# Another order of the steps on all engines of a two-layer gated block, with two waits moved

## The chip, the cores and the metric

The kernel runs on one core of a Trainium2 chip. The metric is the device time of one execution in microseconds. The kernel before takes 654.42 us (median of 3 runs, 654.09 to 656.05).

## The reference

The input is x of 16 sequences with 128 tokens and 256 channels, and a context of 16 x 128 x 64. Two layers follow each other; in each, an attention over the context and a feed-forward network are added to x behind a gate tanh(g), both after a layer norm without weights.

```python
x = x + tanh(g_xattn[0]) * (softmax(q k^T / 4) v @ Wc.T + bc)     # 16 heads of 16, 4 groups of keys
x = x + tanh(g_ffn[0]) * (sparsify_2to4(silu(n @ w_gate) * (n @ w_up)) @ w_down)    # 1024 wide
x = x + tanh(g_xattn[1]) * (softmax(q k^T / sqrt(8)) v)           # 32 heads of 8, 8 groups
x = x + tanh(g_ffn[1]) * (sum over 8 experts of cw * expert(n) + shared expert(n))  # 176 wide
```

q is the normalised x itself, k and v are the context. sparsify_2to4 keeps the two largest of each four. cw holds, for the two experts with the largest biased score, sqrt(softplus(n @ gate_w.T)), and 0 for the rest.

## The kernel before, in words

**Units.** The work is cut into 32 units, one sequence in one layer each. The order of units is a list: four of layer 0, then one of layer 1 and one of layer 0 in turn, then the last four of layer 1. A *pair* is one unit of either layer. What follows calls the unit that comes first "unit 0"; units 0 to 3 are the first four sequences in layer 0.

**Steps.** Each unit's program on an engine is written as four generators (attention_1, attention_2, ffn_1, ffn_2), which yield between steps. `merge` (in front of the engines' programs) gives each step the time 20000·n + t, with n the unit's number in the list and t from the table `TIMES`, sorts all steps of an engine by it, and emits them in that order. The engines run their instructions in this order and wait on semaphores for each other, so `TIMES` sets nothing but the order on each engine. SP's order is not in the table; it is written out at the end of SP's program.

```python
                    steps += [(SLOT * n + t, n, h, run) for t in TIMES[name][h, L]]
            steps += [(TIMES[name][part.__name__][0], -1, 0, part()) for part in once]
            for *_, run in sorted(steps, key=lambda s: s[:3]):
                next(run, None)
```

**TensorE (PE).** In attention_1 it transposes q (L750) and makes the scores for the row maxima (L789); in attention_2 it makes the transposed scores (L818, L819 in layer 0, L821 in layer 1), the weighted sums (L832, 8 or 16 matmuls), turns the result, and in layer 0 projects it (`product`, L742 to L745). In ffn_1 it turns the normalised rows into UP[0], waits for their rounded part and the rest (f_at_hi from ACT L673, f_at_lo from VectorE L1182) in a step of its own (L883 and L884), and makes the gate and up products, in layer 1 those of the shared expert and the router first (L907 to L911). In ffn_2 it turns the hidden rows (hT0, hT1, ..), makes the other experts' products and the down products. Products are in rounded float32, with a rounded part ("hi") and the rest ("lo") of the operands, so that each is two or three matmuls.

**ACT and VectorE (DVE).** ACT copies from PSUM with rounding, takes exponentials (L658) and silu, and for the router Abs and Relu (L689, L690), Exp (L693) and Ln (L696); `prepare`, `round_keys`, `round_up` (L606) and `round_down` (L614) round the weights once. Between Exp, Ln and Silu stands a table load. ao_hi (L666) is the rounded part of the attention's result. VectorE takes maxima (L1092), norms, the low parts, the hidden products; `split_keys` (L1037), `split_up` (L1044) and `split_down` (L1053) make the low parts of the weights once.

**POOL.** It computes reciprocal roots, the low part of q (L471, q_lo), x + b (L480), copies of the values (L485, L493), small router steps, the drop of the sparse values (L515), sets constants (`late_constants`, L436 to L449), and issues two loads on its own DMA queue: `load_w13` (L561, all experts' first weights, 3168 KB) and `load_w2` (L567, L569).

**Keys.** The keys k are rounded and split once. For units 0 and 1 SP copies them straight into place (`first_k0`, L299 and L301). For all others SP first writes them to a scratch in DRAM (`stage_keys`: kd0a twice, L338, kd0b, L340, kd1, L343, with the 1 MB load of w_down, L341, in between) and reads each unit's part from there (`load_k0`, L306 and L308). SP does unit 0's next loads, then stage_keys, then unit 1's next loads and unit 2's keys; before stage_keys it waits until unit 0's value copy on POOL is done (v0_done), because the next load overwrites its source.

Of the kernel before, what the change touches and what calls it, by code (L numbers as in the profile page):

```python
# [31 lines left out]
def flamingo_block(nc, x, ctx_kv, ctx_t, g_x, g_f, wc_t, bc, w_up, w_down, gate_w_t, gate_b, w13, w2, out):  # L32
# [22 lines left out]
    with ctx:  # L55
# [130 lines left out]
        def wait_part(eng, name, n, k):  # L186
# [3 lines left out]
        SLOT = 20000  # L190
        TIMES = {
            "Pool": {
                (0, 0): [-12726, -11933, -8176, 2795, 4595],
                (0, 1): [-14992, -14516, -10388, -1699],
                (1, 0): [19249],
                (1, 1): [20461],
                (2, 0): [36844, 36845, 48715, 48716, 53506],
                (2, 1): [36843, 36844, 39683, 39684, 39685, 40505, 41937, 41938, 41939],
                (3, 0): [57067, 57628, 58227],
                (3, 1): [58491],  # L200
                "one_hot_1": [-11725],
                "late_constants": [24996],
                "load_w13": [61],
                "load_w2": [80360],
            },
            "Act": {
                (0, 0): [521, 2075, 5158],
                (0, 1): [867, 868, 4047, 4048],
                (1, 0): [17463, 19059, 21601, 22294, 25145, 27473, 34511, 36218],
                (1, 1): [18686, 18758, 22595, 23037, 27030, 29353, 30610, 31365, 31366, 31430, 34845, 35181],  # L210
                (2, 0): [48564, 54697, 56775, 59277, 61858],
                (2, 1): [49748, 54795, 55454, 56580, 58664, 59330],
                (3, 0): [60865, 74180, 75237],
                (3, 1): [59488, 61027, 74290, 75390, 75654, 75655, 78503],
                "prepare": [2709],
                "round_keys": [5972],
                "round_up": [38364],
                "round_down": [56819],
            },
# [9 lines left out]
            },  # L229
            "DVE": {  # L230
# [8 lines left out]
                "prepare": [-3234],  # L239
                "split_keys": [17241],  # L240
                "split_up": [41480],
                "split_down": [60289],
            },
        }

# [490 lines left out]
        def _(pe):  # L736
# [127 lines left out]
            def ffn_1(i, L):  # L864
# [15 lines left out]
                wait(pe, "f_norm", n)  # L880
                turn(UP[0], lambda k: f_xn[:, P * k:P * (k + 1)], KT).then_inc(S["f_xt_ps"], 1)
                yield
                wait(pe, "f_at_hi", n)  # L883
                wait(pe, "f_at_lo", n)  # L884
                if L == 0:
                    for c in range(2):
                        yield
                        for b_, off, name in ((0, 0, "f_g"), (1, I0, "f_u")):
                            if b_:
                                yield  # L890
                            if c:
                                wait(pe, "f_h0" if b_ else "f_sg0", n)
                            for k in range(KT):
                                if k:
                                    yield
                                w = slice(off + CH * c, off + CH * (c + 1))
                                last = product(UP[b_][:, :], at_hi[b][:, k, :], at_lo[b][:, k, :],
                                               up_hi[:, k, w], up_lo[:, k, w], k == 0, k == KT - 1)
                            last.then_inc(S[f"{name}{c}"], 1)
                else:  # L900

                    yield
                    c0 = 2 * E * EI
                    for k in range(KT):
                        if k:
# [399 lines left out]
```

## Time and profile before

| | |
|---|---|
| median of 3 runs | 654.42 us |
| profiled execution | 653.18 us |
| its span, first to last instruction | 651.4 us |
| mean granted clock of PE | 0.982 |
| PE busy | 582.7 us, 89% of the span |
| DVE, ACT, POOL busy | 471.9, 436.8, 238.8 us |
| DMA | 21.44 MB, mean 33 GB/s |

The profile is of one execution. A busy time is the sum of an engine's instructions; a wait is an engine's idle time with what ended it. Matmuls overlap in the pipeline, so the spacing of their starts tells more than their durations. The granted clock is a share of 2.4 GHz, and 0.50 is the level of 1.2 GHz. Queue q1 is SP's, q10 is ACT's, q0 is POOL's; all of them run on the core's 16 DMA engines.

### The profile page before, as it was taken

What the parts mean: (1) busy time and instruction counts of PE and PEld (TensorE: products, weight loads), DVE (VectorE), ACT (ScalarE), POOL (GpSimd) and SP (SyncE); (2) the same over time, 40 slices, a digit from 0 to 9 for tenths busy, and PEclk for the clock granted to TensorE, in tenths of its full rate; (3) what the DMA queues carried; (4) which work ended last, traced back from release to release, by engine and by line L of the source; (5) the groups of instructions that cost most, each with busy time, mean ns of one, the idle gap of its engine ahead of it and who ended that gap; (6) DMA issues with size and microseconds to landing.
All of it is one profiled execution on the core that took longest, in us unless ns stands there. A gap on an engine that the chain in (4) does not pass through costs nothing.

```text
span 651.4 us, 10817 instructions
## 1 busy us (share of the span) xinstructions
PE 582.7 (89%) x3552; PEld 450.7 (69%) x3552; DVE 471.9 (72%) x1152; ACT 436.8 (67%) x812; POOL 238.8 (37%) x498
## 2 busy tenths in 40 slices
PE   0654788999999999999999999999999999999886
PEld 0332576777878777777878787777778786767675
DVE  4361878686969788796969697887969696966444
ACT  3251655677786877677777868776777778678952
POOL 5340444261534334251515343351515152341120
PEclk9975999899999999999999999999999999999999
DMA  8752007000000000000000000000000000000000
GB/s 258 217 183 75 4 17 109 18 9 18 14 21 10 22 15 18 10 18 17 17 19 15 20 9 22 14 15 12 18 9 11 8 11 10 12 7 2 10 8 17
DMA packets 24694, 21.44 MB, mean 33 GB/s; under 512 B 9872, under 2 KB 23680, under 8 KB 23744
## 3 DMA queue, kind: packets, MB, share of 16 engines
q1 hardware_dynamic: 21984, 13.04, 7.8%
q0 software_dynamic: 1888, 4.87, 2.5%
q10 hardware_dynamic: 768, 2.85, 1.5%
q8 instruction: 29, 0.48, 0.3%
q14 instruction: 25, 0.20, 0.1%
HBM read 12.61 MB, written 5.24 MB: 27 GB/s over the span
## 4 chain that ended last, share of the span: by engine, by line
PE 66%; ACT 13%; POOL 7%; DVE 6%; issue 5%; DMA 2%; SPq 1%; DVEq 0%; POOLq 0%; ACTq 0%
PE bank L742 12%; PE bank L750 12%; PE bank L745 12%; PE bank L789 8%; PE bank L832 7%; PE bank L744 5%; PE bank L821 4%; ACT L658 3%; POOL rt L547 3%; ACT L696 2%; ACT pt L658 2%; PE bank L818 2%; PE bank L819 2%; DMA k0a<-down_hi 2%; PE bank L911 1%
## 5 line engine op out<-in xcount | busy, mean ns | idle before, releaser
L658 ACT ACTIVATE pt<-bank 128x512 f32<-128x512 f32 x192 | 109.4, 603 | 10.1 <-PE bank L821 5.5
L1092 DVE TENSOR_REDUCE mx<-bank 128x4 f32<-128x512 f32 x128 | 86.1, 684 | 8.3 <-PE bank L789 7.4
L707 ACT ACTIVATE ht_hi<-bank 128x512 fp32r<-128x512 f32 (+1 forms) x96 | 50.4, 543 | 61.4 <-PE bank L750 60.8
L742 PE MATMUL bank<-w_r,at_hi 128*128 128x352 f32 x256 | 88.4, 346 | 3.4 <-DVE work L1200 0.9
L456 POOL TENSOR_SCALAR a_ve<-a_mv 128x1 f32<-128x1 f32 x32 | 9.1, 284 | 214.2 <-DVE a_mv L1062 213.3
L745 PE MATMUL bank<-w_r,at_lo 128*128 128x352 f32 x256 | 82.2, 323 | 0.0
L1137 DVE SCALAR_TENSOR_TENSOR work<-bank,cw,work 128x176 f32<-128x176 f32 x128 | 45.3, 395 | 42.5 <-ACT work L724 28.4
L1092 DVE TENSOR_REDUCE q0b<-bank 128x4 f32<-128x512 f32 x64 | 42.6, 688 | 42.3 <-PE bank L789 42.0
L1231 DVE TENSOR_TENSOR ht_lo<-bank,ht_hi 128x512 fp32r<-128x512 f32 (+1 forms) x96 | 58.0, 618 | 18.4 <-ACT ht_hi L707 18.4
L821 PE MATMUL bank<-qt,k 128*128 128x512 f32 x128 | 54.1, 443 | 7.4 <-DMA qt<-mt 3.3
L742 PEld LDWEIGHTS bank<-w_r,at_hi 128*128 128x128 f32 x256 | 48.4, 189 | 15.3 <-DVE work L1200 5.8
L742 PE MATMUL bank<-up_hi,at_hi 128*128 128x512 f32 x128 | 55.5, 434 | 0.0
L750 PE MATMUL bank<-ident,work 128*128 128x128 f32 x336 | 50.5, 275 | 4.5 <-DVE work L1137 2.5
L789 PE MATMUL bank<-k,qt 128*128 128x512 f32 x128 | 49.7, 426 | 2.2 <-ACT qt L642 1.7
L744 PE MATMUL bank<-up_lo,at_hi 128*128 128x512 f32 x128 | 50.9, 397 | 0.0
L745 PE MATMUL bank<-up_hi,at_lo 128*128 128x512 f32 x128 | 50.7, 396 | 0.0
L742 PE MATMUL bank<-w_r,ht_hi 128*128 128x256 f32 x208 | 50.2, 281 | 0.0
L745 PE MATMUL bank<-w_r,ht_lo 128*128 128x256 f32 x208 | 49.9, 279 | 0.0
L745 PEld LDWEIGHTS bank<-w_r,at_lo 128*128 128x128 f32 x256 | 48.2, 188 | 1.9
L750 PEld LDWEIGHTS bank<-ident,work 128*128 128x128 f32 x336 | 40.2, 141 | 13.4 <-DVE work L1137 3.7
L832 PE MATMUL bank<-pt,v 128*32 128x512 f32 x384 | 48.8, 611 | 0.0
L515 POOL TENSOR_TENSOR work<-work,keep 128x512 f32<-128x512 f32 x32 | 37.3, 1165 | 25.0 <-DVE keep L1168 25.0
(163 smaller groups left out, 1540.7 us busy)
## 6 DMA issues: line engine op xcount, KB each, us to landing
w_r<-in_w POOLq DMA_DIRECT2D x1, 3168.0 KB, 13.8
x<-in_x SPq DMA_DIRECT2D x16, 128.0 KB, 2.2
work<-in_w_up ACTq DMA_DIRECT2D x2, 1024.0 KB, 9.3
k<-kd SPq DMA_DIRECT2D x128, 12.0 KB
out<-y SPq DMA_DIRECT2D x16, 128.0 KB, 1.7
w_r<-in_w POOLq DMA_DIRECT2D x1, 1536.0 KB, 7.1
kd0a<-down_hi SPq DMA_DIRECT2D x2, 512.0 KB
pt<-in_w_down SPq DMA_DIRECT2D x1, 1024.0 KB, 19.3
```

Source lines behind the costliest of these rows:

```text
L658: act.activation(pt[:, g, :], PV[g % 2][:, :], ACT.Exp, scale=float(HD[L]) ** -0.5)\
L707: act.activation(ht_hi[:, 4 * t:4 * t + cols // P, :], DOWN[b][:, 0:cols].rearrange("p (k t) -> p k t", t=P), ACT.Copy)\
L742: pe.matmul(o, a_hi, w_hi, start=first, stop=False, skip_group_check=free)
L744: pe.matmul(o, a_hi, w_lo, start=False, stop=False, skip_group_check=free)
L745: return pe.matmul(o, a_lo, w_hi, start=False, stop=last, skip_group_check=free)
L750: last = pe.transpose(o[:, P * k:P * (k + 1)], src(k), ident[:, :])
L789: pe.matmul(QK[(1 + m) % 2][:, :], qt[b][:, t, P * j:P * (j + 1)], k_[:, 4 * t:4 * t + 4, :].rearrange("p g t -> p (g t)"), start=True, st ...
L821: last = pe.matmul(o, k1[c][:, g, :], qt[b][:, g // 4, :], start=True, stop=True)
L832: last = pe.matmul(PV[0][BLK * g:BLK * (g + 1), :], vv[:, 4 * t + g, :], pt[:, 4 * t + g, :], start=t == 0, stop=t == tiles - 1, skip_grou ...
L1092: dve.tensor_reduce(o, QK[(1 + m) % 2][:, :].rearrange("p (g t) -> p g t", t=T), AX.X, ALU.max, negate=True).then_inc(S["a_r"], step)
L1137: last = dve.scalar_tensor_tensor(out=hid[b][:, EI * e:EI * (e + 1)], in0=o[:, EI * k:EI * (k + 1)], scalar=cw[b][:, e:e + 1], in1=sg[b][: ...
L1231: dve.tensor_tensor(ht_lo[:, r, :], DOWN[b][:, 0:cols].rearrange("p (k t) -> p k t", t=P), ht_hi[:, r, :].bitcast(F32), ALU.subtract).then ...
```

## The change

The table `TIMES` gets other numbers, so that the order changes on PE, ACT, DVE and POOL. The two waits of PE for the split rows move from a step of their own to the step of the first product that reads them. No operation is added or removed. The part of the table that the text speaks of, and the moved waits:

```diff
         TIMES = {
             "Pool": {
-                (0, 0): [-12726, -11933, -8176, 2795, 4595],
-                (0, 1): [-14992, -14516, -10388, -1699],
+                (0, 0): [-15000, -14999, -10496, -1576, -1575],
+                (0, 1): [-12565, -12564, -9814, -5533],
...
-                "one_hot_1": [-11725],
-                "late_constants": [24996],
-                "load_w13": [61],
-                "load_w2": [80360],
+                "one_hot_1": [-14199],
+                "late_constants": [-7829],
+                "load_w13": [16839],
+                "load_w2": [22346],
...
             "Act": {
...
-                (1, 0): [17463, 19059, 21601, 22294, 25145, 27473, 34511, 36218],
+                (1, 0): [11579, 16631, 18206, 20385, 21777, 22019, 24894, 29235],
...
-                (2, 1): [49748, 54795, 55454, 56580, 58664, 59330],
+                (2, 1): [42225, 47367, 51807, 53210, 55296, 56805],
...
-                "prepare": [2709],
-                "round_keys": [5972],
-                "round_up": [38364],
-                "round_down": [56819],
+                "prepare": [1023],
+                "round_keys": [7257],
+                "round_up": [12373],
+                "round_down": [45546],
...
             "PE": {
-                (0, 0): [-559, 1533, 1773, 3821, 8011],
+                (0, 0): [-3011, 3429, 4743, 6848, 8003],
...
-                (1, 0): [12633, 16179, 17889, 19242, 20545, 22954, 25084, 28315, 30810, 30811],
+                (1, 0): [13189, 13757, 15851, 17195, 20380, 22309, 26401, 27950, 30027, 30300],
...
-                (2, 0): [40913, 43206, 43207, 44676, 46174, 50799, 51022, 52507, 52737, 53443],
-                (2, 1): [41823, 44672, 44836, 44837, 52109, 52264, 56478, 56479],
-                (3, 0): [62720, 62721, 67431, 67482, 69795, 69922, 70871],
+                (2, 0): [41161, 44330, 45550, 47182, 49606, 49786, 51148, 52503, 53285, 53383],
+                (2, 1): [41709, 44728, 45305, 47205, 51933, 52514, 55943, 55944],
+                (3, 0): [57444, 60603, 67366, 67649, 68973, 70573, 70574],
...
             "DVE": {
...
-                "prepare": [-3234],
-                "split_keys": [17241],
-                "split_up": [41480],
-                "split_down": [60289],
+                "prepare": [-2515],
+                "split_keys": [13618],
+                "split_up": [22778],
+                "split_down": [58931],
...
                 turn(UP[0], lambda k: f_xn[:, P * k:P * (k + 1)], KT).then_inc(S["f_xt_ps"], 1)
                 yield
-                wait(pe, "f_at_hi", n)
-                wait(pe, "f_at_lo", n)
                 if L == 0:
                     for c in range(2):
                         yield
+                        if c == 0:
+                            wait(pe, "f_at_hi", n)
+                            wait(pe, "f_at_lo", n)
...
                 else:
 
                     yield
+                    wait(pe, "f_at_hi", n)
+                    wait(pe, "f_at_lo", n)
```

Read as an order, with the steps at the start in which the two kernels differ most:

- POOL before: unit 0's root and q_lo, load_w13, unit 0's x + b and values, unit 1's root, q_lo, x + b and values, late_constants, unit 2. After: unit 0's root and q_lo, late_constants, unit 0's x + b and values, unit 1's root and q_lo, load_w13, unit 1's x + b and values, load_w2, unit 2. Before, load_w2 stands where the fifth unit begins.
- ACT before: round_up stands behind unit 0's ao_hi, round_down in unit 0's ffn_1, behind unit 1's ao_hi. After: round_up stands ahead of unit 0's attention_2, round_down between unit 1's attention result and its ao_hi.
- DVE before: split_keys behind unit 1's normalisation, split_up ahead of unit 0's second normalisation. After: split_keys ahead of unit 1's normalisation, split_up behind it and ahead of unit 1's maxima.
- PE before: unit 2's first two score products stand ahead of unit 1's weighted sums. After: behind them.
- In a pair later on, PE before: layer 0's last transposed scores, then the new layer 1 unit's first two score products, its turned rows and the old unit's first turned hidden half. After: that half directly behind the transposed scores. ACT before: Abs and Relu of the router, the second half's rounding, the router's Exp, ao_hi, Ln. After: the second half's rounding, Abs and Relu, ao_hi, Exp, Ln.

## Rows read from the trace of the kernel before

**Rows 1.** Busy time by stage; then PE's granted clock, DMA share, GB/s
```profile
42.50:58.00 15.50, 3.36 (x10) 1.74 (x10) 4.74 (x6) 2.77 (x6) 4.89 (x5) 0.61 0.41 135
80.00:540.00 460.00, 447.54 (x2802) 353.46 (x2801) 363.57 (x898) 331.37 (x623) 183.06 (x375) 1.00 0.08 18
540.00:651.40 111.40, 96.82 (x605) 74.88 (x604) 68.36 (x185) 74.34 (x140) 26.80 (x62) 1.00 0.03 9
```

**Rows 2.** The chain of waits, 0 to 80 us: start us, us, what
```profile
9.17 11.04 DMA k0a<-down_hi
...
47.94 10.12 issue
```

**Rows 3.** Timeline of SP's queue: start us, us of issuing, operation
```profile
18.30 0.59 SPq L301 DMA_DIRECT2D k0b<-down_lo  x1
...
24.70 1.26 SPq L338 DMA_DIRECT2D kd0a<-down_hi  x2
...
47.70 1.20 SPq L306 DMA_DIRECT2D k0a<-kd0a  x1
```

**Rows 4.** DMA queues, 14 to 22 us: packets, MB, share of 16 engines
```profile
q0 software_dynamic: 244, 3.09, 95.3%
q1 hardware_dynamic: 244, 0.15, 24.3%
q10 hardware_dynamic: 141, 0.04, 9.4%
```

**Rows 5.** DMA queues, 22 to 24 us
```profile
q1 hardware_dynamic: 638, 0.16, 37.2%
```

**Rows 6.** DMA queues, 26 to 28 us
```profile
q1 hardware_dynamic: 14, 0.11, 26.7%
```

**Rows 7.** DMA issues: what, KB each, us from issue to landing
```profile
w_r<-in_w POOLq DMA_DIRECT2D x1, 3168.0 KB, 13.8
...
w_r<-in_w POOLq DMA_DIRECT2D x1, 1536.0 KB, 7.1
```

**Rows 8.** Timelines of DVE and ACT: weights split and rounded; start us, us
```profile
40.81 4.99 DVE L1044 TENSOR_TENSOR up_lo<-work,up_hi 128x2048 fp32r<-128x2048 f32 x2
...
67.53 1.90 ACT L614 ACTIVATE down_hi<-pt 128x2048 fp32r<-128x2048 f32 x1
```

**Rows 9.** Timeline of PE behind the second gate; idle time before in brackets
```profile
59.19 1.94 PE L832 MATMUL bank<-pt,v 128*32 128x512 f32 x8
...
73.17 0.50 PE L818 MATMUL bank<-qt,k0a 128*128 128x512 f32 x1 [1.57 <-ACT pt L658]
...
77.52 0.41 PE L750 MATMUL bank<-ident,f_xn 128*128 128x128 f32 x2 [2.31 <-DVE f_xn L1066]
```

**Rows 10.** Timeline of PE, one pair of units
```profile
313.91 0.40 PE L818 MATMUL bank<-qt,k0a 128*128 128x512 f32 x1
314.14 0.40 PE L819 MATMUL bank<-qt,k0b 128*128 128x512 f32 x1
314.58 0.70 PE L789 MATMUL bank<-k,qt 128*128 128x512 f32 x2
...
350.42 0.70 PE L789 MATMUL bank<-k,qt 128*128 128x512 f32 x2
```

**Rows 11.** Waits of PE's weight loads, 160 to 520 us: us, times, longest
```profile
PEld bank L821 <- DMA qt<-mt: 5.3, 10, 0.5
...
PEld bank L742 <- DVE work L1200: 3.9, 10, 0.4
PEld bank L821 <- ACT pt L658: 3.4, 10, 0.4
```

**Rows 12.** Timeline of ACT, the router of one unit
```profile
320.23 0.20 ACT L693 ACTIVATE rt<-rt 128x8 f32<-128x8 f32 x1
320.89 0.38 ACT L666 ACTIVATE ao_hi<-bank 128x256 fp32r<-128x256 f32 x1 [0.46 <-PE bank L750]
321.30 1.28 ACT L696 ACT_TABLE_LOAD   x1
```

More of the change, by code:

```diff
@@ L192, in flamingo_block @@
             "Pool": {
-                (0, 0): [-12726, -11933, -8176, 2795, 4595],
-                (0, 1): [-14992, -14516, -10388, -1699],
[L195 to L200, printed above, removed]
-                "one_hot_1": [-11725],
-                "late_constants": [24996],
@@ L203, in flamingo_block @@
-                "load_w13": [61],
-                "load_w2": [80360],
+                (0, 0): [-15000, -14999, -10496, -1576, -1575],
+                (0, 1): [-12565, -12564, -9814, -5533],
+                (1, 0): [18632],
+                (1, 1): [11838],
+                (2, 0): [31094, 31095, 47595, 49321, 50573],
+                (2, 1): [30923, 30924, 37097, 37098, 37289, 37438, 37589, 41658, 43145],
+                (3, 0): [55922, 56685, 56686],
+                (3, 1): [50053],
+                "one_hot_1": [-14199],
@@ L205, in flamingo_block @@
+                "late_constants": [-7829],
+                "load_w13": [16839],
+                "load_w2": [22346],
             },
             "Act": {
-                (0, 0): [521, 2075, 5158],
-                (0, 1): [867, 868, 4047, 4048],
-                (1, 0): [17463, 19059, 21601, 22294, 25145, 27473, 34511, 36218],
-                (1, 1): [18686, 18758, 22595, 23037, 27030, 29353, 30610, 31365, 31366, 31430, 34845, 35181],
-                (2, 0): [48564, 54697, 56775, 59277, 61858],
@@ L212, in flamingo_block @@
-                (2, 1): [49748, 54795, 55454, 56580, 58664, 59330],
-                (3, 0): [60865, 74180, 75237],
-                (3, 1): [59488, 61027, 74290, 75390, 75654, 75655, 78503],
-                "prepare": [2709],
-                "round_keys": [5972],
-                "round_up": [38364],
-                "round_down": [56819],
+                (0, 0): [-2525, -2524, 2141],
+                (0, 1): [-2580, -1918, 1054, 1178],
+                (1, 0): [11579, 16631, 18206, 20385, 21777, 22019, 24894, 29235],
@@ new lines, in flamingo_block @@
+                (1, 1): [11053, 16063, 19285, 22101, 22212, 22832, 24053, 24054, 25522, 25758, 27915, 28572],
+                (2, 0): [42310, 50008, 53019, 56531, 58415],
+                (2, 1): [42225, 47367, 51807, 53210, 55296, 56805],
+                (3, 0): [59841, 63075, 66082],
+                (3, 1): [57130, 58962, 65811, 68905, 71876, 72168, 73704],
+                "prepare": [1023],
+                "round_keys": [7257],
+                "round_up": [12373],
+                "round_down": [45546],
```

22 rows, old and new, of the table TIMES are left out of this document.

## The prediction, made before the changed kernel ran

> **What bounds the kernel now.** I read the busy times by stage first, then the chain of waits of the start and the DMA queues there, and last one period of the steady stage.
>
> TensorE is the engine with the least idle time, and that idle time is what can be won. The stages tell where it lies [rows 1]: from 80 to 540 us it lacks 460 − 447.5 = 12.5 us, at the end 14.6 us, and in the 15.5 us before 58 us it works for 3.4 us only. The chain of the start names two gates [rows 2]: 11.04 us until the first unit's keys land (TensorE resumes at about 20.3 us), and 10.12 us in which TensorE waits, until 58.06 us, for the keys of the third unit, the first that come back from the scratch in DRAM.
>
> The second gate is a queue. SP issues the last piece of unit 1's keys at 18.30 us, but the first copy of all keys to the scratch only at 24.70 us and the third unit's keys at 47.70 us [rows 3]; they stand behind the copies and the 1 MB of the down projection. What such a queue does beside another one shows in the stage from 14 to 22 us, when the big expert load (w13, 3168 KB) runs on POOL's queue: 244 packets of it moved, and 244 packets of SP's queue [rows 4]. The DMA engines take turns, one packet each, whatever their size. A w13 packet held an engine for 0.953·8·16/244 = 0.50 us; as soon as w13 had landed, SP's queue moved 638 packets in 2 us [rows 5].
>
> The copy to the scratch does not use all engines: from 26 to 28 us, when it runs alone, 14 packets took 26.7% of 16 engines, that is 4.3 engines at 0.61 us a packet [rows 6]. So a mean DMA share of 0.41 before the gate [rows 1] may be a few engines that are never free.
>
> **The change, part by part.** It reorders the steps; no operation is added or taken away, the matmuls and table loads stay as many.
>
> *First gate.* On POOL, w13 moves from before unit 0's sum x+b to behind unit 1's q_lo, so that by the walk it is issued at about 24 us instead of ahead of the first gate. The up weights are through by 14 us (ACT's queue moved only 0.04 MB after that [rows 4]). Some 200 packets of the first keys, a part of the 244 and 141 of SP's and ACT's queues, were then left, and with nothing big to take turns with they need under 1 us [rows 5]: the gate opens at about 15.4 us, −4.9 us. SP gains the same: unit 0's value copy no longer waits for a late load, and SP goes on at 18.9 us, where its own issuing ends. The key copies start at 19.8 instead of 24.70 us: −4.9 us. Three more steps go ahead here and are counted at nothing: the late constants on POOL, because unit 0's value copy must only be done by 18.9 us; rounding the up weights on ACT, because its next step waits for unit 0's last maximum, near 19 us; the split of the keys ahead of unit 1's normalisation, because TensorE has the third unit's keys to wait for in the end. If that wait went, they would cost some 5 us of unit 1's start.
>
> *w13 beside the key copies.* This is what the move pays. w13 now runs from about 29 us, in the middle of the copies. It has 3168 KB in 256 rows of 12.4 KB, a packet each, 16 an engine. On an engine that the copies keep busy, each takes its 0.50 us out of turn: +8.0 us. Ends: 0, if the copies' engines have gaps enough, and 8.0. I take 8.0: packet for packet is what [rows 4] show.
>
> *w2 beside them.* The second expert load moves from far behind, where the fifth unit begins, to close behind w13. It is 1536 KB in 1 KB packets and took 7.1 us from issue to landing [rows 7], on all engines. Behind w13 in its queue it meets the rest of the copies, the down weights and the keys, packet for packet: between 0 and 7.1 us, and I take 4.0, since on the busy engines most of what it meets is left by then.
>
> The gate before the third unit's keys thus goes from 58.06 to 58.06 − 4.9 + 8.0 + 4.0 = 65.2 us: **+7.1 us**. SP's queue is behind in any case; TensorE, with less to wait for earlier, stands there from about 43 us.
>
> The Trainium skill ("DMA: Bandwidth & Descriptors", section on queues, rings and completion order) says that each engine goes round its queues by packets, which agrees with the equal counts. In its section on why a semaphore rises by 16 it says that a DMA from SP uses as many engines, up to 16, as divide the outer dimension on both sides: four for the copy with four groups outside, and the 4.3 engines agree. Its fit of 2.0 us plus bytes over 436 GB/s would give, as an estimate, 10.9 us of transfer for both loads spread over all engines, and with that in place of the 12.0 us the kernel would come to 656.4 us.
>
> *Behind the gate.* The weighted sums of unit 1 now stand before the gate, in the wait. They took 1.94 us [rows 9] right behind a stretch with a mean granted clock of 0.61 [rows 1]; I count half of it, for at the gate other products run at that clock in their place. Rounding the down weights, 1.90 us on ACT [rows 8], moves into the wait too; it held up the exponentials for which TensorE waited 1.57 us. The next wait, 2.31 us for unit 1's normalised rows [rows 9], hangs on VectorE's chain with the split of the down weights in it, which stays where it was; so the two don't add. What is late next is this chain, and it starts about 1.4 us sooner: −1.4 us, between 0 and −3.5. Splitting the up weights, 4.99 us on VectorE [rows 8], goes ahead of the gate; its cover is the wait for the keys, and without that cover it would cost those 5 us at unit 1's maxima.
>
> *Steady stage.* A pair of units takes 350.42 − 314.58 = 35.84 us [rows 10]; 80 to 540 us is 12.8 pairs. Small waits stand in each: for the maxima's row by DMA 0.5, VectorE's product 0.4, the exponentials 0.3 [rows 11], and 0.2 us ahead of a unit's first scores (314.58 − 314.14 = 0.44, where such products follow each other by 0.23 [rows 10]); 1.4 us a pair. Walking through the new order with these durations: the turn of the old unit's hidden half now stands before the new unit's first scores and fills one (−0.2); unit 1's q moves ahead of two products and a tie of VectorE ahead of the normalisation, which fills some of the third (−0.2). Against it, the router's exponential moves behind ao_hi on ACT: it ran at 320.23, and the table load at 321.30 followed ao_hi directly [rows 12]; now its 0.20 us come in between, on the chain that ends in the first and second wait (+0.15). The two waits of TensorE, for the split rows, now stand at the first product that reads them. Left at their own step they would hold the two score products that the new order puts in between, and with them the maxima on VectorE; by themselves they give nothing, for in the old order next to nothing stood there. Sum −0.2 a pair, **−2.6 us** in all; at best the whole 1.4 us a pair, −18 us; at worst one more 0.5 us wait a pair, +6.4 us.
>
> *End.* The last units keep their order but for neighbours: 0, ±1.5 us.
>
> **Sum:** +7.1 − 1.4 − 2.6 = +3.1 us. The profiled execution's span of 651.4 becomes 654.5 us, with the 1.8 us around it 656.3; the median of the three runs stands 1.2 us over that execution (654.42 to 653.18), so 657.5 us.
>
> **The rivals.**
> (a) *The loads fit into free engine time, faster.* The mean DMA share of 0.41 before the gate speaks for it, the 4.3 engines against it. Then 8.0 and 4.0 vanish, the gate is at 53.2 us, and the time is 654.42 − 4.9 − 1.4 − 2.6 = 645.5 us. It decides if less than 6.9 of the 12 us are in the way: below that the kernel is faster by over 0.3%. Chance 0.15 for all of it, 0.08 for about half (651.5).
> (b) *The new order takes out half of the steady waits*, −9.5 instead of −2.6: 650.6 us. For it: TensorE's producers have room (ACT works for 331 and VectorE for 364 of 460 us [rows 1]). Against: their waits hang on chains, not on load. 0.12.
> (c) *ACT's chain gets late*: the exponential behind ao_hi, and the wait at the product that needs sgs grows by 0.5 us a pair: +6.4 instead of −2.6, 666.5 us. 0.13.
> (d) *The order changes nothing that binds* in the steady stage; the start alone gives 660.1 us. That belongs to my forecast's spread.
>
> **How the numbers follow.** The forecast with its spread (654 to 661) has 0.52. A measurement tells apart about 0.3%, 2.0 us. Of the forecast 0.35 are slower, 0.16 the same, 0.01 faster; (c) is slower; (a) is faster, its half mostly the same or faster; (b) is faster or the same. Faster 0.28, same 0.24, slower 0.48. The range of 8 in 10 leaves out (a) in full and the far end of (c): 648 to 664 us.
>
> **What would show it.** Right: TensorE's first scores near 15.4 us; w13 issued near 24 us; TensorE idle from about 43 to 65 us, with the third unit's keys landing last; in the stage of that wait POOL's and SP's queues with equal packet counts; 2 us or more less idle behind the gate; a pair of 35.4 to 35.9 us. Wrong: a gate before 58 us (then the copies' engines had room), or a pair shorter than 35.2 or longer than 36.2 us.

## The result, and the profile after the change

The changed kernel takes 658.04 us (median of 6 runs, 657.44 to 658.61) where the kernel before takes 655.77 us (6 runs, 654.09 to 656.84): a ratio of 1.0039, 95% interval 1.0022 to 1.0055. It is 2.3 us slower; 3.1 us had been forecast.

The traced executions are further apart, since that of before (653.18 us) is shorter than any of its six runs: spans of 651.4 and 656.3 us. Where the 4.9 us between them arise can be read off three products that both traces have: the third unit's first scores, and the weighted sums of the sixth and of the 28th unit, 11 pairs apart.

| from | to | before | after | difference |
|---|---|---|---|---|
| start | third unit's first scores | 58.06 us | 66.89 us | +8.8 us |
| these | sixth unit's weighted sums | 78.62 us | 76.09 us | -2.5 us |
| these | 28th unit's weighted sums | 394.40 us | 392.18 us | -2.2 us |
| these | end of the span | 120.3 us | 121.1 us | +0.8 us |

The timelines that the table is made from. TensorE before (L832 is the weighted sum, and the third unit's scores stand in the chain of [rows 2]):

```profile
136.68 1.06 PE L832 MATMUL bank<-pt,v 128*32 128x512 f32 x8
...
531.08 1.07 PE L832 MATMUL bank<-pt,v 128*32 128x512 f32 x8
```

After:

```profile
16.59 1.19 PE L789 MATMUL bank<-k0a,qt 128*128 128x512 f32 x2 [5.06 <-DMA k0a<-down_hi]
...
66.89 1.19 PE L789 MATMUL bank<-k0a,qt 128*128 128x512 f32 x2 [21.36 <-issue]
...
142.98 1.06 PE L832 MATMUL bank<-pt,v 128*32 128x512 f32 x8
...
535.16 1.06 PE L832 MATMUL bank<-pt,v 128*32 128x512 f32 x8
```

The reader sees the first gate open at 16.59 instead of 20.30 us, and the second at 66.89 instead of 58.06 us: TensorE now stands there for 21.36 us (10.12 before, [rows 2]). "Issue" is what the profile calls a wait for which it finds no releaser; the last of the third unit's keys lands at 66.80 us, 0.09 us earlier. The timeline of SP's queue after the change, to be held against [rows 3]:

```profile
20.00 1.26 SPq L338 DMA_DIRECT2D kd0a<-down_hi  x2
...
25.99 19.53 SPq L343 DMA_DIRECT2D kd<-down_hi  x2
...
52.08 2.03 SPq L306 DMA_DIRECT2D k0a<-kd0a  x1
```

And POOL's timeline, with the issues of w13 and of the larger part of w2:

```profile
26.95 0.98 POOL L561 DMA_DIRECT2D w_r<-in_w  x1
...
29.88 1.06 POOL L567 DMA_DIRECT2D w_r<-in_w  x1
```

SP starts the copies of the keys 4.7 us earlier, but the first read of the third unit's keys is issued 4.4 us later. In between SP takes 19.53 us to issue two of the copies to kd1 (11.74 us before); the profile does not say why, and that its queue took no more is a reading. The stages, against [rows 1] (PE's granted clock is the third number from the right):

```profile
42.50:58.00 15.50, 2.62 (x13) 0.96 (x11) 0.42 (x1) 2.56 (x5) 0.00 (x0) 0.61 0.63 176
58.00:66.00 8.00, 0.00 (x0) 0.00 (x0) 0.00 (x0) 1.82 (x1) 0.00 (x0) 0.50 0.35 94
...
80.00:540.00 460.00, 446.66 (x2794) 352.10 (x2793) 363.36 (x901) 330.85 (x625) 183.96 (x373) 0.99 0.05 15
540.00:656.30 116.30, 103.07 (x637) 80.88 (x635) 73.18 (x192) 78.41 (x147) 30.05 (x68) 0.99 0.03 9
```

From 58 to 66 us every engine stands but ACT, which rounds the down weights (L614) from 64.18 us on, while the DMA engines are busy for 0.35 of the time only. That a few of them have most of the work fits the 4.3 engines of [rows 6], but it is argued: the profile does not say on which engine a packet ran. The DMA queues after the change from 32 to 36 us, in the middle of w13 (packets, MB, share of 16 engines):

```profile
q0 software_dynamic: 103, 1.31, 81.6%
q1 hardware_dynamic: 34, 0.23, 21.5%
```

The counts are not equal as in [rows 4]: at least 69 of w13's packets took no turns with SP's. Nor are they equal in TensorE's wait itself: from 45.5 to 66.9 us POOL's queue moved 452 packets, most of them of w2, and SP's 2075.

A pair of units on TensorE's timeline, against [rows 10]:

```profile
319.73 0.40 PE L819 MATMUL bank<-qt,k0b 128*128 128x512 f32 x1
319.96 0.60 PE L750 MATMUL bank<-ident,work 128*128 128x128 f32 x4
320.32 0.71 PE L789 MATMUL bank<-k,qt 128*128 128x512 f32 x2
...
355.96 0.71 PE L789 MATMUL bank<-k,qt 128*128 128x512 f32 x2
```

ACT's timeline in the router, against [rows 12]:

```profile
326.19 0.38 ACT L666 ACTIVATE ao_hi<-bank 128x256 fp32r<-128x256 f32 x1 [0.43 <-PE bank L750]
326.47 0.20 ACT L693 ACTIVATE rt<-rt 128x8 f32<-128x8 f32 x1
326.69 1.28 ACT L696 ACT_TABLE_LOAD   x1
```

The turn of the old unit's hidden half starts 0.23 us after the last transposed scores, as one such product after the other, and the new unit's scores follow it 0.36 us later: the slack in the 0.44 us of [rows 10] is filled. On ACT the Exp (L693) now stands between ao_hi and the table load. A pair takes 355.96 - 320.32 = 35.64 us instead of 35.84.

### The profile page after: what moved, and what is told of

The parts are those of the page before. It is cut to its first block, busy times and chain, and to the rows that moved or that the text cites. A ratio compares the mean times of both kernels' runs of the same rounds, so it can differ in the third digit from the quotient of the medians.

```text
span 656.3 us, 10816 instructions
## 1 busy us (share of the span) xinstructions
PE 583.3 (89%) x3552; PEld 454.9 (69%) x3552; DVE 471.3 (72%) x1152; ACT 436.1 (66%) x812; POOL 240.6 (37%) x498
## 4 chain that ended last, share of the span: by engine, by line
PE 64%; DVE 11%; POOL 9%; ACT 8%; issue 6%; DMA 1%; SPq 1%; DVEq 0%; POOLq 0%; ACTq 0%
PE bank L750 12%; PE bank L742 12%; PE bank L745 11%; PE bank L832 7%; PE bank L789 7%; PE bank L744 5%; PE bank L821 3%; POOL rt L547 3%; ACT L696 2%; PE bank L818 2%; PE bank L819 2%; DVE work L1140 2%; DVE f_xn L1069 2%; POOL a_rs L459 1%; PE bank L914 1%
## 5 line engine op out<-in xcount | busy, mean ns | idle before, releaser
L456 POOL TENSOR_SCALAR a_ve<-a_mv 128x1 f32<-128x1 f32 x32 | 10.6, 332 | 232.3 <-DVE a_mv L1065 231.3
L742 PE MATMUL bank<-w_r,at_hi 128*128 128x352 f32 x256 | 90.3, 354 | 4.6 <-DVE work L1203 1.0
L1095 DVE TENSOR_REDUCE mx<-bank 128x4 f32<-128x512 f32 x128 | 83.8, 677 | 9.6 <-PE bank L789 9.5
L745 PE MATMUL bank<-w_r,at_lo 128*128 128x352 f32 x256 | 82.1, 322 | 0.0
L1140 DVE SCALAR_TENSOR_TENSOR work<-bank,cw,work 128x176 f32<-128x176 f32 x128 | 45.3, 396 | 40.5 <-ACT work L724 27.0
L821 PE MATMUL bank<-qt,k 128*128 128x512 f32 x128 | 56.7, 446 | 4.9 <-DMA qt<-mt 3.1
L750 PE MATMUL bank<-ident,work 128*128 128x128 f32 x336 | 53.0, 277 | 4.9 <-DVE work L1140 3.0
L789 PE MATMUL bank<-k,qt 128*128 128x512 f32 x128 | 51.1, 440 | 1.0 <-ACT qt L642 0.6
L832 PE MATMUL bank<-pt,v 128*32 128x512 f32 x384 | 48.7, 609 | 1.8 <-ACT pt L658 1.6
L789 PE MATMUL bank<-k0a,qt 128*128 128x512 f32 x64 | 25.8, 448 | 27.0 <-issue 21.4
```

The source lines that it names most:

```text
L742: pe.matmul(o, a_hi, w_hi, start=first, stop=False, skip_group_check=free)
L745: return pe.matmul(o, a_lo, w_hi, start=False, stop=last, skip_group_check=free)
L750: last = pe.transpose(o[:, P * k:P * (k + 1)], src(k), ident[:, :])
L789: pe.matmul(QK[(1 + m) % 2][:, :], qt[b][:, t, P * j:P * (j + 1)], k_[:, 4 * t:4 * t + 4, :].rearrange("p g t -> p (g t)"), start=True, st ...
L821: last = pe.matmul(o, k1[c][:, g, :], qt[b][:, g // 4, :], start=True, stop=True)
L832: last = pe.matmul(PV[0][BLK * g:BLK * (g + 1), :], vv[:, 4 * t + g, :], pt[:, 4 * t + g, :], start=t == 0, stop=t == tiles - 1, skip_grou ...
```

## The experiments

The theory was the prediction's: the two expert loads beside the copies of the keys make the second gate late, the new order of the other engines gains a little, and the balance is the difference of the two. The rivals were that the loads fit into free engine time, that the order makes the gate late, and that single steps are worth other amounts than the sum had. They ran in three groups, each on one chip. The kernel before, run beside them, spread from 648.2 to 658.9 us there (medians 653.43, 653.02 and 652.96 us; beside the result its six runs lay within 2.8 us), so times tell apart a few us only; for fractions of a us the traces are read: the gate is the start of the third unit's first scores, and a pair is 1/11 of the time between the weighted sums of the sixth and the 28th unit.

| kernel | us | ratio to before (95%) | gate, us | pair, us |
|---|---|---|---|---|
| old_order_new_loads | 661.19 | 1.0111 (1.0057 to 1.0165) | 64.25 | 35.84 |
| new_order_old_loads | 647.16 | 0.9895 (0.9844 to 0.9947) | 56.75 | 35.64 |
| new_order_w2_back | 650.94 | 0.9969 (0.9941 to 0.9997) | 61.25 | 35.64 |
| new_order_w13_late | 644.71 | 0.9865 (0.9816 to 0.9915) | 53.47 | 35.63 |
| late_waits_own_step | 651.03 | 0.9954 (0.9921 to 0.9986) | 54.94 | 36.07 |
| late_hT0_back | 649.21 | 0.9942 (0.9903 to 0.9981) | 54.65 | 35.81 |
| late_exp_ahead | 652.45 | 0.9975 (0.9939 to 1.0012) | 54.49 | 35.54 |
| late_keys_split | 634.17 | 0.9724 (0.9675 to 0.9773) | 45.32 | 35.63 |
| changed_keys_split | 642.92 | 0.9855 (0.9798 to 0.9912) | 52.31 | 35.64 |
| old_keys_split | 642.11 | 0.9843 (0.9783 to 0.9903) | 48.45 | 35.85 |
| old_w13_behind_xb | 650.66 | 0.9966 (0.9923 to 1.0009) | 53.16 | 35.86 |
| split_exp_ahead | 632.03 | 0.9681 (0.9614 to 0.9748) | 45.69 | 35.54 |

### Loads and order apart

The old order with the loads at their new steps:

```diff
-                "late_constants": [24996],
-                "load_w13": [61],
-                "load_w2": [80360],
+                "late_constants": [60],
+                "load_w13": [12000],
+                "load_w2": [24996],
```

> The order of the kernel before; only the three POOL steps (late constants, w13, w2) stand where the change puts them. Theory (the two expert loads beside the key copies make the second gate, whatever the order): first scores near 16.6 us, third unit's keys land near 66.9 us as after the change (58.06 before), a pair stays at 35.85 us, time 655.8 + 8.8 = 664.6 us (663 to 667). Rival (the new order of the other engines makes the late gate, the loads fit in free engine time): gate at 53 us, 650 us.

The new order with both loads at their old steps:

```diff
-                "load_w13": [16839],
-                "load_w2": [22346],
+                "load_w13": [-9000],
+                "load_w2": [80360],
```

> The changed kernel with both expert loads back at their old places (w13 behind unit 0's q_lo, w2 where the fifth unit begins). Theory: first scores near 20.3 us, third unit's keys at 58.1 us, behind that the order's own gain of 1.4 us and 0.2 us a pair: 655.8 - 4.0 = 651.8 us (649 to 653). Rival (the new order gains nothing, the trace of after just stood high or low): 655.8 us.

The new order with w2 alone put back:

```diff
-                "load_w2": [22346],
+                "load_w2": [80360],
```

> The changed kernel with w2 alone back where the fifth unit begins; w13 stays behind unit 1's q_lo. Theory of the prediction's sum (w13 costs 8.0 us and w2 4.0): third unit's keys at 66.9 - 4.0 = 62.9 us, 654.0 us. Rival A (w2 is nothing, it uses idle engines): 658 us. Rival B (w2's small packets cost its full 7.1 us): 651 us.

And the new order with w2 back and w13 behind unit 3's value copy:

```diff
-                "load_w13": [16839],
-                "load_w2": [22346],
+                "load_w13": [58426],
+                "load_w2": [80360],
```

> The changed kernel with w13 issued behind unit 3's value copy (about 89 us, its first product stands at 144 us) and w2 at its old place. Theory: first scores near 16 us, key copies alone from 20 us as they ran from 24.7 us before, so the third unit's keys at 58.1 - 4.7 = 53.4 us and the time 658.0 - 13.5 = 644.5 us (643 to 648). Rival (the copies are late by themselves, or w13 beside the loads of later units holds those up): 650 us or more.

The third unit's first scores on TensorE's timeline (its wait in brackets), in old_order_new_loads:

```profile
64.25 1.19 PE L789 MATMUL bank<-k0a,qt 128*128 128x512 f32 x2 [19.89 <-issue]
```

In new_order_old_loads:

```profile
56.75 1.19 PE L789 MATMUL bank<-k0a,qt 128*128 128x512 f32 x2 [11.57 <-issue]
```

In new_order_w2_back:

```profile
61.25 1.19 PE L789 MATMUL bank<-k0a,qt 128*128 128x512 f32 x2 [15.25 <-issue]
```

In new_order_w13_late:

```profile
53.47 1.19 PE L789 MATMUL bank<-k0a,qt 128*128 128x512 f32 x2 [5.28 <-issue]
```

The gate goes with the loads, under either order. In the new order, taking w2 away from the copies moves it from 66.89 to 61.25 us: w2 costs 5.6 us. Taking w13 away too moves it to 53.47: w13 costs 7.8 us. What is left is the copies themselves: 33.5 us from their first issue (19.99 us) to the gate, as in the kernel before (24.70 to 58.06, 33.4 us). In times the loads cost 661.19 - 653.43 = 7.8 us in the old order, and the order gains 653.43 - 647.16 = 6.3 us with the old loads; the interval has the 4.0 us expected in it. Of the 6.3 us, 1.3 are the gate, at 56.75 instead of 58.06 us: the key copies start at 21.82 us there. That rival (a) is wrong is shown by this. With both loads out of the way the changed kernel is faster than the one before by 1.35%.

Two runs did not come out as expected. The gate and the time of old_order_new_loads are lower than the 66.9 us and 663 to 667 us: with the loads at the same steps and the key copies from 20.0 us on, the gate is at 64.25 us in the old order and at 66.89 in the new one. So the new order does make the gate later, by 2.6 us. POOL comes to w13 at 25.14 us in the old order and at 26.95 in the new one; that this is the reason was not tested. Against old_w13_behind_xb (below), whose copies start at 20.05 us, the two loads cost the old order 64.25 - 53.16 = 11.1 us at the gate, not 13.4. And the 650.94 us of new_order_w2_back are rival B's 651 us rather than the 654.0 us of the theory; its gate, with 5.6 us, lies between the two, and the kernel before ran 2.3 us shorter on that chip than beside the result.

### The order's parts in a pair

Three kernels undo one step each, on the base of new_order_w13_late. TensorE's waits in a step of their own again (in either layer):

```diff
                 yield
+                wait(pe, "f_at_hi", n)
+                wait(pe, "f_at_lo", n)
                 if L == 0:
                     for c in range(2):
                         yield
-                        if c == 0:
-                            wait(pe, "f_at_hi", n)
-                            wait(pe, "f_at_lo", n)
...
                     yield
-                    wait(pe, "f_at_hi", n)
-                    wait(pe, "f_at_lo", n)
```

> Base is the changed kernel with both loads late (pair 35.63 us, 8.7 us under the kernel before). Here TensorE's two waits for the split rows stand again in a step of their own. Theory of the prediction (left there they hold the score products that the new order puts in between, and the maxima behind them): a pair of 35.7 to 36.0 us, 1 to 5 us slower than the base. Rival (split rows are ready by then, moving the waits is worth nothing): a pair of 35.63 us, same time as the base.

The turned hidden half behind the new unit's first scores (TensorE, layer 0):

```diff
-                (3, 0): [57444, 60603, 67366, 67649, 68973, 70573, 70574],
+                (3, 0): [57444, 61710, 67366, 67649, 68973, 70573, 70574],
```

> Same base; one step of TensorE goes back: the old unit's first turned hidden half stands behind the new unit's first two scores and turned rows, as before the change. Theory (that turn fills the 0.2 us ahead of a unit's first scores): a pair of 35.83 us, as the kernel before, 2.6 us slower than the base. Rival (the 0.2 us a pair come from other places of the order): a pair of 35.63 us.

The router's Abs, Relu and Exp ahead (ACT, layer 1):

```diff
-                (2, 1): [42225, 47367, 51807, 53210, 55296, 56805],
+                (2, 1): [42225, 46000, 48000, 53210, 55296, 56805],
```

> Same base; on ACT the router's Abs, Relu and Exp stand again ahead of ao_hi (Abs and Relu ahead of the second half's rounding too), as before the change. Theory of the prediction (Exp behind ao_hi costs 0.15 us a pair on the chain to the maxima's row and the shared silu): a pair of 35.48 us, 1.9 us faster than the base. Rival (Exp there lies on no chain that binds): a pair of 35.63 us, same time.

The weighted sums on TensorE's timeline that bound the 11 pairs, in the base, new_order_w13_late:

```profile
127.33 1.06 PE L832 MATMUL bank<-pt,v 128*32 128x512 f32 x8
...
519.23 1.07 PE L832 MATMUL bank<-pt,v 128*32 128x512 f32 x8
```

In late_waits_own_step:

```profile
132.01 1.06 PE L832 MATMUL bank<-pt,v 128*32 128x512 f32 x8
...
528.82 1.06 PE L832 MATMUL bank<-pt,v 128*32 128x512 f32 x8
```

In late_hT0_back:

```profile
133.66 1.06 PE L832 MATMUL bank<-pt,v 128*32 128x512 f32 x8
...
527.62 1.06 PE L832 MATMUL bank<-pt,v 128*32 128x512 f32 x8
```

In late_exp_ahead:

```profile
130.92 1.06 PE L832 MATMUL bank<-pt,v 128*32 128x512 f32 x8
...
521.82 1.07 PE L832 MATMUL bank<-pt,v 128*32 128x512 f32 x8
```

Against the base's 391.90 / 11 = 35.63 us, the hidden half back costs 0.19 us a pair, where the whole change gains 0.20. As the later Exp costs 0.09 us (below), other steps must give about 0.1 us a pair; the prediction's other gain, unit 1's q and the tie of VectorE (0.2 us), was not tested. The waits in their own step cost 0.44 us a pair (36.07 us, just over the 35.7 to 36.0 expected), more than the new order gains; the view of the weight loads' waits of late_waits_own_step, from 160 to 520 us (us, times, longest), names the place, the score products, two in each pair. The base has no such row; the kernel before has it with 13.0 us, so it gives the place and not the amount:

```profile
PEld bank L789 <- issue: 8.2, 20, 0.5
```

So in the new order the moved waits are what makes the rest pay; moved alone, in the old order, they were not run. The Exp ahead gains 0.09 us a pair (0.15 had been expected), yet the kernel got slower, not faster, and its trace says where: 81.0 us from the weighted sums of the 28th to those of the last unit instead of 78.0, and 48.2 instead of 41.7 us of span behind these. ACT's timeline of late_exp_ahead in the last units:

```profile
605.44 1.28 ACT L693 ACT_TABLE_LOAD   x1
...
606.96 1.28 ACT L724 ACT_TABLE_LOAD   x1
...
612.14 1.28 ACT L696 ACT_TABLE_LOAD   x1
```

And TensorE's waits there from 540 us on (us, times, longest):

```profile
PE bank L750 <- DVE work L1140: 9.2, 4, 3.1
```

In the last units, where no unit of layer 0 runs beside, the step Exp had moved ahead of a silu of the unit before it: Exp, silu, Ln, each with a table load, 17 loads ahead of that silu instead of 14. One number serves all units of a layer, and what helps in a pair hurts at the end. TensorE's wait in that row is 3.0 us in the base.

### What the copies of the keys cost by themselves

```diff
                 for a in range(2):
-                    sp.dma_start(kd0a[:, a], kh.bitcast(F32)).then_inc(S["scratch_k0"], 16)
+                    for g in range(G0):
+                        sp.dma_start(kd0a[g, a], kh[HD0 * g:HD0 * (g + 1), :].bitcast(F32))\
+                            .then_inc(S["scratch_k0"], 16)
...
-                sp.wait_ge(S["scratch_k0"], 16 * 3)
+                sp.wait_ge(S["scratch_k0"], 16 * (2 * G0 + 1))
```

The same edit was put on three kernels: on new_order_w13_late,

> Same base; each of the two copies of the keys to kd0a is issued as four DMAs, one for each group of keys, instead of one with the four groups outside. Theory (the copy of four groups keeps about four DMA engines busy, and these are the gate; a copy of one group's 16 rows spreads over all): third unit's keys land at 41 to 47 us instead of 53.4, TensorE, which has work until 44.5 us, hardly waits, 7 to 9 us faster than the base. Rival (the memory or the queue bounds the copies, not the number of engines): gate stays at 52 to 54 us.

on the changed kernel as it is,

> The changed kernel as it is (w13 issued at about 27 us, w2 at 30), with each copy of the keys to kd0a issued as four DMAs. With both loads late the same split put the landing of the third unit's keys at 43.6 us and the time 2.8% under the kernel before. Theory (on a DMA engine that has key packets waiting the loads' packets go in turn, w13's 16 of 0.50 us among them): the loads still cost most of their 13.4 us, keys land at 52 to 57 us, 643 to 648 us on a chip where the kernel before takes 653. Rival (the loads cost only because about four engines were overfull; on even engines they fit in between): keys land at 44 to 47 us, 634 to 638 us.

and on the kernel before:

> The kernel before, only with each copy of the keys to kd0a issued as four DMAs. Theory: the second gate was these copies' four engines; from the first copy's issue at 24.7 us the third unit's keys need 23.6 us as in the split kernel with late loads (20.0 to 43.6), so they land at 48 us and TensorE, which comes there at 47.9 us, does not wait: 9 to 10 us faster than the kernel before. Rival (w13 until 23 us has already delayed everything else that TensorE waits for there): 3 us faster or less.

The timeline of SP's queue in late_keys_split:

```profile
20.01 4.46 SPq L339 DMA_DIRECT2D kd0a<-down_hi  x8
...
32.70 1.51 SPq L306 DMA_DIRECT2D k0a<-kd0a  x1
```

Its DMA queues from 24 to 26 us:

```profile
q1 hardware_dynamic: 82, 0.34, 74.5%
```

The third unit's first scores on its TensorE:

```profile
45.32 0.73 PE L791 MATMUL bank<-k0a,qt 128*128 128x512 f32 x2
```

The same in changed_keys_split:

```profile
52.31 1.19 PE L791 MATMUL bank<-k0a,qt 128*128 128x512 f32 x2 [6.94 <-issue]
```

And in old_keys_split:

```profile
48.45 1.19 PE L791 MATMUL bank<-k0a,qt 128*128 128x512 f32 x2 [0.24 <-issue]
```

Issued by groups, the copies to kd0a land between 20.0 and 27.3 us; as two DMAs they took from 20.0 to 40.5 us in the base. They moved 0.11 MB in 2 us with 26.7% of the engines' time [rows 6], and now 0.34 MB with 74.5%. SP issues on 10.5 us earlier, TensorE's wait is gone, and the kernel is 2.8% faster than before, where the base is 1.35% faster. The rule of the Trainium skill that the prediction cites ("DMA: Bandwidth & Descriptors", section on why a DMA increments its semaphore by 16) is borne out: 16 rows outside use more engines than four groups. The loads, put beside the split copies again, cost 52.31 - 45.32 = 7.0 us at the gate, and more of the keys themselves: the third unit's land at 52.22 instead of 43.57 us, 8.7 us later, part of it hidden by TensorE's work until 45.3 us. So they are not free here either, though they cost about two thirds of their 13.4 us. The copies to kd1, with eight groups outside, were split in no run; an even load of all engines was not tested. In the kernel before, the split alone takes away 9.6 us of the gate, and TensorE hardly waits there any more (0.24 us).

### The first gate

```diff
-                "load_w13": [61],
+                "load_w13": [2796],
```

> The kernel before, only with w13 one step later on POOL, behind unit 0's x+b: its issue goes from 9.58 to about 11 us, its first packet from 13.9 to about 15.5. Theory (the first gate is a race of w13's first packets with the first keys, which cannot flow before the up weights are through at about 14.6 us; w13 needs no large move): first scores at 16.4 us instead of 20.3, key copies issued at 22 to 23 us, third unit's keys at 56 to 57 us, 1 to 2 us faster. Rival (w13 holds the keys up wherever it is issued in this stretch): first scores at 20 us or later, no faster.

First scores and gate of this kernel on TensorE:

```profile
16.56 1.19 PE L789 MATMUL bank<-k0a,qt 128*128 128x512 f32 x2 [5.02 <-DMA k0a<-down_hi]
...
53.16 1.19 PE L789 MATMUL bank<-k0a,qt 128*128 128x512 f32 x2 [9.18 <-issue]
```

The first gate opens at 16.56 us, as expected; the key copies start at 20.05 us already (22 to 23 expected), and the second gate is earlier than expected (56 to 57). The median is 2.3 us lower, but the interval reaches over 1, so in time this is inconclusive. Two other runs show that the gate of 20.30 us is not even a property of the kernel before. old_keys_split has the same instructions as before up to 24 us, w13 at its old step among them. Its POOL issues w13 here:

```profile
10.25 0.98 POOL L563 DMA_DIRECT2D w_r<-in_w  x1
```

And its TensorE has the first scores here:

```profile
17.05 1.19 PE L791 MATMUL bank<-k0a,qt 128*128 128x512 f32 x2 [5.51 <-DMA k0a<-down_hi]
```

ACT issued its DMAs 0.6 us slower in that execution, so q_lo and with it w13 came at 10.25 instead of 9.58 us and its first packet at 14.60 instead of 13.94 us, when the keys had already been let through. new_order_old_loads, with w13 at 10.24 us, has its first scores at 16.35 us. So of the three traces with w13 at its old step only one has the late first gate, and whether it was the one step on POOL that opened it in old_w13_behind_xb stays open. How often the kernel before falls on either side was not measured; it would be one reason for its spread.

### Both gains together

The split copies, both loads late, and Exp ahead of ao_hi but so close that no silu of the last units comes between Exp and Ln:

```diff
-                (2, 1): [42225, 47367, 51807, 53210, 55296, 56805],
+                (2, 1): [42225, 46000, 49000, 53210, 55296, 56805],
```

> The changed kernel with both loads late and the copies to kd0a split (634.2 us), and on ACT the router's Abs, Relu and Exp ahead of ao_hi, but Exp close ahead of it, so that in the last four units no silu stands between Exp and Ln (the run with Exp further ahead had 17 instead of 14 table loads ahead of the shared silu, all three in the last units). Theory (Exp ahead of ao_hi is worth 0.09 us a pair; those three table loads and the waits behind them were what that run lost at its end): pair 35.54 us, 14 such table loads, 633 us. Rival (the early Exp itself delays the last units): pair 35.54 us and 636 us or more.

The weighted sums on its TensorE that bound the 11 pairs:

```profile
119.67 1.06 PE L834 MATMUL bank<-pt,v 128*32 128x512 f32 x8
...
510.59 1.06 PE L834 MATMUL bank<-pt,v 128*32 128x512 f32 x8
```

A pair of 35.54 us and 14 such table loads, 632.03 us: 3.2% under the kernel before, and the fastest of all. The Exp itself does not delay the last units: from the weighted sums of the 28th to those of the last it takes 78.0 us, and 42.9 us behind these (78.0 and 43.1 in late_keys_split). Beside late_keys_split (634.17 us, 2 runs) the 2.1 us are near the 1.0 us that 11 pairs make, but within the scatter.

## Why the prediction was right

**First gate, -4.9 us.** Right for SP (24.70 to 20.00, -4.7), short for TensorE (20.30 to 16.59, -3.7, where 15.4 us was forecast), and wrong in its cause for TensorE. The step that failed is "the gate opens at about 15.4 us" because w13 is gone: with w13 back at its old step it opens at 16.35 us. By the traces the 20.30 us of before was a race lost by some 0.6 us, which is argued. For the sum this did not matter, since the second gate hangs on SP.

**w13, +8.0 us.** Measured 7.8, in the new order; w13 was issued at 26.95 us (24 expected). The packet count was right, and so was its condition, an engine that the copies keep busy. The sign named for it was wrong: elsewhere w13 ran alone (103 against 34 packets), so the equal counts were not there. That its packets waited in turn on the copies' engines is argued, from 7.8 against 16 x 0.50 us.

**w2, +4.0 us.** Mis-sized: 5.6 us, inside the bounds of 0 and 7.1. With w13 that makes 13.4 us for both in the new order and 11.1 us in the old one, where the sum had 12.0. The prediction's estimate by the fit of the Trainium skill ("DMA: Bandwidth & Descriptors", section on the anatomy of one DMA), 10.9 us (11.05 by the KB of [rows 7]), is further off in the new order and nearer in the old one; it is for loads spread over all engines, and the copies that they meet are not spread.

**The gate** was to come at 65.2 us and came at 66.89, and TensorE stood from 45.5 us on (43 expected).

**Behind the gate, -1.4 us.** Measured -2.5, inside 0 to -3.5, but not the same with every place of the loads. With the old loads it is 78.62 to 76.25 us (new_order_old_loads), -2.4. With the new loads it is 82.05 (old_order_new_loads, 64.25 to 146.30 us) to 76.09 us: -6.0, beyond the range. The sum counted the order at nothing at the gate, where it costs 2.6 us, and at too little behind it, where it had not priced the granted clock either (below). These misses run against each other, so that +2.3 us came out beside +3.1 is in part luck.

**Steady stage, -0.2 us a pair.** Measured 0.20, and the parts that were tested were nearly right: 0.19 for the hidden half (0.2), 0.09 lost by the Exp (0.15). The third part, 0.2 us by unit 1's q and the tie, was not tested; the sum leaves it about 0.1. That the waits at the first product save the score products of the new order was right, with 0.44 us a pair as its size; that they give nothing by themselves is not shown.

**End, 0 +- 1.5 us.** +0.8.

Of the rivals, (a) is excluded by the load experiments, (b) and (c) by the pair of 35.64 us, (d) by its 0.20 us. Half of 1.4 us in 12.8 pairs is 9.0 us and not the 9.5 of (b); this changes nothing.

## What to carry to other kernels

Before a big load is moved "out of the way", look at what its queue will meet at the new place: beside copies that keep a few DMA engines full, w13 cost 7.8 us, nearly its 16 x 0.50 us of packets an engine. A mean DMA share of 0.4 with every engine waiting can mean that few DMA engines have the work; look then at the outer dimension of the DMA, for here splitting one copy by groups was worth 1.6% by itself (old_keys_split), as much as the new order with both loads out of the way (1.35%), and both together 2.8%. And where one table of steps serves all units, look at the last units apart: a step that gains 0.1 us in each pair cost over 9 us there.

## What was not expected of the hardware

Behind the wait TensorE's clock was low for a while. The stages behind the gate after the change (granted clock third from the right):

```profile
66.00:80.00 14.00, 12.39 (x52) 9.71 (x52) 9.19 (x21) 6.00 (x10) 3.07 (x7) 0.80 0.06 15
80.00:110.00 30.00, 26.66 (x146) 19.25 (x145) 23.70 (x50) 16.64 (x31) 12.72 (x24) 0.89 0.05 14
```

One of these stages in new_order_w13_late, which waited 5.28 us only:

```profile
66.00:80.00 14.00, 11.04 (x70) 8.24 (x69) 11.60 (x21) 7.92 (x15) 5.93 (x10) 1.00 0.30 105
```

After the change the clock stands at its lower level, 1.2 GHz, in the last 8 us of the wait (0.50), and is mixed from both levels until 110 us; in the other kernel it is at 2.4 GHz from 66 us on. The stretch from the gate to the sixth unit's weighted sums takes 76.1 us in the first and 73.9 us in the second, with the same order. In the old order it takes 78.6 us before and 82.1 us in old_order_new_loads, which waited 19.89 us and had 0.87 from 66 to 80 us; its sixth unit's weighted sums:

```profile
146.30 1.06 PE L832 MATMUL bank<-pt,v 128*32 128x512 f32 x8
```

The length of the wait does not tell the cost, though. late_exp_ahead waited 6.85 us only; its gate, and the stage from 66 to 80 us:

```profile
54.49 1.19 PE L789 MATMUL bank<-k0a,qt 128*128 128x512 f32 x2 [6.85 <-issue]
...
66.00:80.00 14.00, 11.06 (x51) 6.89 (x51) 10.76 (x19) 7.14 (x13) 7.41 (x13) 0.76 0.15 46
```

Its stretch takes 130.92 - 54.49 = 76.4 us, as much as behind the 21.36 us. The stages from 66 to 80 us do not hold the same work in each kernel, since the gates differ. That the clock makes these differences is argued from the rows; no run changed it alone.

Also not expected: SP stood for long in issuing. The two DMAs to kd1 took 19.53 us to issue after the change, 11.74 us before and 3.11 us with the split copies, and everything behind them in SP's program waited for that. That its queue was full is argued.
